# The product of edge weight and one-hot, for building the hop matrix, moved from VectorE to ScalarE

## The reference

```
h = relu(layernorm(x)); x = x + normalize(segment_sum(h[src] @ W_msg + b) + h @ W_self + b')   # layer 0
h = relu(layernorm(x)); x = x + segment_sum(h[src] @ W_rel[edge_type])                         # layer 1
h = relu(layernorm(x)); emb, acc = h, h                                                        # layer 2
for _ in range(3):
    emb = segment_sum(edge_weight[:, None] * emb[src], dst); acc = acc + emb
x = x + acc / 4
h = relu(layernorm(x)); x = x + edge_mlp_layer(h, edge_attr, ...)                              # layer 3
```

## Time and profile before

| | |
|---|---|
| time, median of 3 runs | 9690.01 us (9684.74 to 9692.3) |
| time of the profiled execution | 9684.6 us |
| its span | 9682.9 us |
| VectorE busy over the span | 4792.0 us (49%) |
| ScalarE busy over the span | 1117.6 us (12%) |
| TensorE, mean granted clock over the span | 0.603 of full |

### The profile page before, as it was taken

One profiled execution on the slowest core, in us unless ns is written; L12 is line 12 of the kernel. 1 busy time (PEld: TensorE's weight loads), 2 busy tenths in 40 slices (PEclk: granted clock), 3 DMA queues, 4 the chain that ended last, 5 costly groups with the idle time before them and its releaser, 6 DMA issues.

```text
span 9682.9 us, 125475 instructions
## 1 busy us (share of the span) xinstructions
PE 7196.8 (74%) x38567; PEld 5277.0 (54%) x38568; DVE 4792.0 (49%) x10473; ACT 1117.6 (12%) x2676; POOL 5005.8 (52%) x5265
## 2 busy tenths in 40 slices
PE   2477777777778763333334777777999999999999
PEld 1366666666664663333332222223777777777777
DVE  2599999999992972222222000001444444444444
ACT  1111111111122110000000000001111111111111
POOL 0376666666642767777774111110655555555554
PEclk9555566556655555555556999998555555555555
DMA  5654444445443531111115999996222222222222
GB/s 105 94 96 95 96 96 94 94 95 97 94 87 131 98 75 26 26 26 26 26 26 192 426 403 426 402 426 276 62 60 58 60 58 59 59 58 59 59 60 50
DMA packets 841613, 1176.30 MB, mean 121 GB/s; under 512 B 676431, under 2 KB 696335, under 8 KB 813858
## 3 DMA queue, kind: packets, MB, share of 16 engines
q1 hardware_dynamic: 668850, 923.61, 29.5%
q0 software_dynamic: 172528, 250.20, 12.0%
HBM read 921.76 MB, written 258.23 MB: 122 GB/s over the span
## 4 chain that ended last, share of the span: by engine, by line
PE 40%; DVE 19%; POOL 13%; DMA 13%; issue 13%; DVEq 2%; SPq 1%; ACT 0%; POOLq 0%; ACTq 0%
POOL arena L470 13%; DMA arena<-B_d 10%; PE ps L932 8%; PE ps L875 8%; DVE ps L1178 6%; DVE arena L1179 5%; PE ps L890 4%; PE ps L873 4%; PE ps L951 4%; PE ps L923 4%; DVE arena L1181 4%; DVE pair L1154 3%; PE ps L944 2%; PE ps L773 2%; PE ps L816 2%
## 5 line engine op out<-in xcount | busy, mean ns | idle before, releaser
L470 POOL DMA_INDIRECT arena<-tab,idx x4992 | 4757.9, 953 | 3001.9 <-issue 1582.2
L816 PE MATMUL ps<-arena 128*128 128x64 f32 x6656 | 1400.0, 398 | 1066.2 <-DMA arena<-tab,idx 1064.1
L802 PE MATMUL ps<-arena 128*64 128x98 f32 x15872 | 1457.3, 359 | 696.6 <-DVE arena L1181 695.2
L816 PEld LDWEIGHTS ps<-arena 128*128 128x128 f32 x6656 | 1338.9, 307 | 1136.2 <-issue 1064.9
L802 PEld LDWEIGHTS ps<-arena 128*64 128x64 f32 x15872 | 1181.5, 211 | 938.1 <-DVE arena L1181 794.5
L890 PE MATMUL ps<-arena,ev 128*64 128x512 f32 (+1 forms) x4836 | 1106.4, 603 | 369.7 <-DMA arena<-B_d 294.3
L1154 DVE TENSOR_TENSOR X<-X,ps 128x64 f32 x1664 | 368.1, 221 | 1536.5 <-PE ps L816 1154.3
L890 PEld LDWEIGHTS ps<-arena,ev 128*64 128x64 f32 x4836 | 385.4, 143 | 1090.5 <-issue 738.9
L1179 DVE TENSOR_TENSOR arena<-arena,ps 128x784 f32<-128x784 f32 x992 | 956.9, 965 | 0.0
L932 PEld LDWEIGHTS ps<-arena 128*128 128x128 f32 x3328 | 725.8, 331 | 334.4 <-issue 331.6
L875 PEld LDWEIGHTS ps<-pair,arena 128*128 128x128 f32 x3328 | 725.0, 330 | 312.9 <-issue 312.9
(11 more groups left out here) (201 smaller groups left out, 4406.2 us busy)
## 6 DMA issues: line engine op xcount, KB each, us to landing
arena<-B_d SPq DMA_DIRECT2D x186, 3136.0 KB, 17.1
B_d<-stg SPq DMA_DIRECT2D x248, 784.0 KB
arena<-tab,idx POOLq DMA_INDIRECT x4992
arena<-rel_d SPq DMA_DIRECT2D x208, 256.0 KB, 3.3
tab<-arena SPq DMA_DIRECT2D x26, 1024.0 KB, 3.9
attr_s<-arena SPq DMA_DIRECT2D x13, 512.0 KB, 12.2
attrG<-attr_s SPq DMA_DIRECT2D x208, 32.0 KB, 2.9
rec_d<-arena SPq DMA_DIRECT2D x6, 832.0 KB, 23.9
```

The lines of the kernel that those rows point to most:

```text
L470: pool.indirect_dma_start(gat[:, r, k * width:(k + 1) * width], None, table, bass.IndirectOffsetOnAxis(ap=idx[:, r, k:k + 1], axis=0)).the ...
L802: ins = pe.matmul(ps[3 + j % 2][a * KP:(a + 1) * KP, i2 * KC:(i2 + 1) * KC], Lw[:, j % 2, t, :], Rc[:, j % 2, t, :], start=True, stop=True)
L816: ins = pe.matmul(ps[6 + r % 2][:, k * D:(k + 1) * D], S[:, r % 2, k, :], gat[:, r, k * D:(k + 1) * D], start=True, stop=True)
```

## The change

VectorE no longer multiplies the first one-hot by the edge weights. ScalarE does it in `weighted`, in eight ACTIVATEs (function Copy) for a part, one for each of its eight record tiles, with the weight as a factor for each partition. It reads the one-hot from the PSUM bank and writes Lw. The function is called for part 0 ahead of the loop over a quarter's parts, and for part j + 1 ahead of `matrix_part` of part j, so that it stands in ScalarE's order behind the idx copy of the quarter and before L633 of the part ahead.

VectorE's first one-hot now waits for `lhs_ok` up to the part two back (whose copies read that PSUM bank), its second one for `bmm` as before; the second one signals a new semaphore, `rc_ok`, and TensorE waits for it beside `lhs_ok`, which ScalarE now signals.

```diff
+            def weighted(c, h, r, j):
+
+                u = c * SUBS + (r * QS + j)
+                act.wait_ge(s_["ohp_ok"], u + 1)
+                wait(act, s_["bmm"], u - 1)
+                ohp = ps[2 + 3 * (j % 2)][:].rearrange("p (s k) -> p s k", s=G)
+                s0 = 2 * P + (r * QS + j) * G
+                for t in range(G):
+                    ins = act.activation(Lw[:, j % 2, t, :], ohp[:, t, :], ACT.Copy, scale=cols[:, h, s0 + t:s0 + t + 1])
+                ins.then_inc(s_["lhs_ok"], 1)
...
                         if build:
+                            weighted(c, h, r, 0)
                             for j in range(QS):
+                                if j + 1 < QS:
+                                    weighted(c, h, r, j + 1)
                                 matrix_part(c, r, j)
...
                 pe.wait_ge(s_["lhs_ok"], c * SUBS + (r * QS + j + 1))
+                pe.wait_ge(s_["rc_ok"], c * SUBS + (r * QS + j + 1))
...
+                wait(dve, s_["lhs_ok"], u - 1)
+                dve.tensor_tensor(ohp, column(0, KP), iota_view(0, KP), ALU.is_equal).then_inc(s_["ohp_ok"], 1)
                 wait(dve, s_["bmm"], u - 1)
-                dve.tensor_tensor(ohp, column(0, KP), iota_view(0, KP), ALU.is_equal).then_inc(s_["ohp_ok"], 1)
-                dve.tensor_tensor(Rc[:, j % 2, :, :], column(1, KC), iota_view(0, KC), ALU.is_equal)
-                dve.wait_ge(s_["ohp_ok"], u + 1)
-                dve.tensor_tensor(Lw[:, j % 2, :, :], ohp, column(2, KP), ALU.mult).then_inc(s_["lhs_ok"], 1)
+                dve.tensor_tensor(Rc[:, j % 2, :, :], column(1, KC), iota_view(0, KC), ALU.is_equal).then_inc(s_["rc_ok"], 1)
```

More of the change, by code:

```diff
@@ L221, in gnn_kernel @@
             proj_mv nrm_in nrm_out idx_ok pc_ok rec2_out beg_oh beg_ps off_in off_ps tile_in tile_ps iota_ok
-            tix_ok row_d wm_ok recT cols_ok ohp_ok lhs_ok bmm bev l1_done emb_ok emb_out hop_mm sum_ok ev_a ev_d
+            tix_ok row_d wm_ok recT cols_ok ohp_ok rc_ok lhs_ok bmm bev l1_done emb_ok emb_out hop_mm sum_ok ev_a ev_d
             hop_T ag_a ag_d
```

## The result

| | before | changed |
|---|---|---|
| time, median | 9689.9 us | 9801.0 us |
| lowest to highest of 4 runs | 9684.7 to 9692.3 | 9795.6 to 9816.6 |
| profiled execution, its span | 9682.9 | 9799.0 |

The change makes the kernel slower: ratio 1.0118, 95% interval 1.0100 to 1.0136, that is 111 us. The forecast was slower by 242 us (9932), with a range from 9680 to 10150.

A forecast was written before the change was run, and what follows sets the result against it. VectorE was taken to bound the build at 47.8 us a chunk. The new ring gives 51.9, so 62 chunks add 254 us; less 10 for TensorE's clock, that is 9932 us, range 9680 to 10150.

The forecast's parts named there:

- the ring: Per quarter: ScalarE waits for segment products, weights, TensorE multiplies the parts, then the next segment products; 51.9 us a chunk.
- w0: ScalarE's eight ACTIVATEs weighting part 0, behind the idx copy; claimed from 0.32 to 2.02 us after the segment products' end.
- the relief: VectorE loses 992 L1181 of 0.60 us, 2.4 us a quarter; 420 us less if nothing else moved in.
- w1: ScalarE's eight ACTIVATEs weighting part 1; claimed to end 3.72 us after the segment products' end.
- w2: ScalarE's eight ACTIVATEs weighting part 2; claimed to end 5.81 us after the segment products' end.
- w3: ScalarE's eight ACTIVATEs weighting part 3; claimed to end at 7.90 us, last result at 8.00, after the segment products' end.
- second wait, rc_ok: TensorE's added wait for VectorE's second one-hot, counted in the ring at 0.1 us a quarter.
- I take 10 us off: TensorE's clock: runs at the higher level may become somewhat commoner; 10 us off, giving 9932.
- if L816's mean falls well under 3.2: Sign that the prediction is wrong: segment products averaging well under 3.2 us; 3.17 was taken.
- The cover: VectorE's work between waits fits in its slack; L1159 to L1164 and its 3 us loop return lie mostly inside.
- The operand's read hides: Rival: ScalarE's factor read adds nothing to the pitch, eight ACTIVATEs take 0.88 us, TensorE sets the ring; 9390 us; 11%.
- TensorE warms: Rival: part 3 and L816 run at TensorE's higher clock level, a chunk of 45 us, some 9500 us; 4%.

The follow-up runs named there:

- Experiment 4: The kernel before with L1181 left out and the first one-hot written straight to Lw, edge weights left out: 9314.0 us, ratio 0.9619.
- experiment 10: The changed kernel with the idx copy and its wait moved behind the weighting of part 0 only: 9476.6 us, 0.9771 of the kernel before.
- Experiment 1: The changed kernel with the idx copy and its wait moved behind the weighting of parts 0 and 1: 9438.9 us, 0.9749 of the kernel before.
- experiments 2: The changed kernel with nine ACTIVATEs a part instead of eight, the extra one writing an unread spare tile: 10101.6 us, 1.0431 of the kernel before.
- experiment 5: The changed kernel with four small unread products on TensorE between a quarter's segment products and part 0: 9732.6 us, 1.0062 of the kernel before.
- experiment 3: The changed kernel with an immediate factor 1.0 instead of the per-partition operand, edge weights left out: 9312.5 us, 0.9618 of the kernel before.
- kernel 6: The changed kernel with two of a part's eight record tiles weighted on VectorE, idx copy still first: 9508.0 us, 0.9824 of the kernel before.
- kernels 7: The changed kernel with two of eight tiles weighted on VectorE and the idx copy behind w1: 9435.0 us, 0.9751 of the kernel before.
- 9: The changed kernel with one of eight tiles weighted on VectorE and the idx copy behind w1: 9381.2 us, 0.9678 of the kernel before.
- 11: The changed kernel with one of eight tiles weighted on VectorE and the idx copy behind w0: 9368.1 us, 0.9667 of the kernel before.

## Why the prediction was right and where it was wrong

**Right: VectorE bound the build**, and once it is relieved the gathers stand next at 10.3. Experiment 4 shows it: 9314, where the prediction's 420 us off the profiled 9685 give 9265 for a build at exactly the gathers' pace.

**Right: the ring.** The prediction said that ScalarE's idx wait puts w0 behind the segment products, and that this outweighs the relief. Experiment 1 shows it by moving the wait behind w0 and w1, experiment 10 by moving it behind w0 alone. The two engines' loads (735 and 697 of 1000) bound nothing.

**Wrong in size: the terms of the ring.** Means over 161 quarters of the changed kernel between 600 and 2600 us, from the end of L816 (after: L831):

| step | predicted | measured |
|---|---|---|
| first ACTIVATE of w0 | 0.32 | 0.38 (mostly 0.28) |
| one ACTIVATE to the next | 0.213 | 0.199 |
| w0 to w1 | 1.70 | 1.59 |
| w1 to w2 (with L633 and its wait for part 0) | 2.09 | 2.27 |
| w2 to w3 | 2.09 | 1.95 |
| part 3 starts | 8.06 | 8.07 |
| second wait, rc_ok | 0.10 | 0 |
| part 3 | 1.46 | 1.32 |
| segment products begin, with L793's share | 9.85 | 9.48 |
| segment products | 3.17 | 2.94 |
| quarter | 12.97 | 12.42 |

All that ScalarE does up to part 3 came out within 0.01 us, but by errors that cancel, which is luck: the ACTIVATEs follow each other more closely (16 in 3.40 us), L633 waits for part 0 instead of coming just right, and w0 starts 0.06 later. The step that failed is what follows it, the working for TensorE: "a part is 488.2/335 = 1.46 us on average", "263.7/83.3 = 3.17 us on average" and "I take 10 us off" for the clock. Both means were taken from the kernel before, where L816 and the parts were not in the ring, and were held as if the engine's clock belonged to the instruction. Part 3 and the segment products, 4.63 us in the sum, measured 4.26: 0.37 x 248 quarters = 92 us, where 10 were allowed. The prediction had named the sign for it: "if L816's mean falls well under 3.2". Half of part 3's share was there to be read before: 1.46 is the mean of all four parts, and part 3 alone took 1.39 in the kernel before (167 quarters between 600 and 2600 us). That the two shorten because the clock is higher is in their durations: a part at 0.89 and at 1.57 us, segment products from 1.90 to 3.68, in the same kernel. That the clock answers to the ring's timing is what experiments 2 and 5 show from both sides: a ring 0.54 longer lowered it and cost 0.7 more, fillers raised it and gave 54 to 68 us back. Why a given quarter runs at one level or the other is not shown. The mean over the whole stretch (0.59 before, 0.62 after) hides this: what counts is the clock during part 3 and L816 alone.

The allowance for rc_ok, 0.1 x 248 = 25 us, was the second miss: TensorE's part 3 starts 0.05 us after w3's last result, as before behind L1181. A further 0.14 a quarter is in the start of L816 (after: L831): 0.07 before part 3's modelled end where no transposes stand between, and the transposes add 0.15 on average, not 0.23. Against these, the prediction's sum has a slip of its own: its terms 8.06, 1.46, 0.1 and 3.17 give 12.79, where it wrote 12.75, so with L793 the column of terms adds up to 13.02 and the 12.97 was 0.05 too low. Together 0.37 + 0.10 + 0.14 - 0.01 - 0.05 = 0.55, or 136 us. The sum before the 10 for the clock was 254; less 136 it is 118, against 116 in the spans, of which 107 lie in the build, and 111 in the medians.

**The operand's price.** The Trainium skill, "ScalarE: Activation LUTs", section "What ACT_TABLE_LOAD costs", has 93 ns for each pointer operand and 93 ns of overlap. The first agrees with experiment 3 (0.20 against 0.10 us in the pitch, from 0.198 and 0.105); by its fixed part of 280 ns the pitch would be 0.24, an estimate from that page, and the trace has 0.20, with 314 ns for the first of a row, where the earlier trace rows gave 313. The sum had it from the rows.

**The cover.** VectorE's slack was there (1472.66 of 2000 busy), though not in every quarter: in 16 of 161 w0 waits for its one-hot, 4.2 us in all. One thing in it was seen otherwise: its loop's return, 3.00 us of idle time before L1140, is not hidden in slack but gone: in the changed kernel L1155, the same one-hot, has 4.1 us of such idle time in 1000, where L1140 had 30.7 (the rows below, the kernel before first). In kernel 6, whose VectorE has more instructions in the loop again, it is back at 2.96 before L1155, and kernels 7, 9 and 11 have it too (2.9 to 3.3 us), which is some 0.37 a quarter.

```profile
L1140 DVE TENSOR_TENSOR arena<-relT,ps 128x1024 f32<-128x1024 f32 x83 | 101.4, 1221 | 34.0 <-issue 30.7 <-PE ps L816 3.1
```

```profile
L1155 DVE TENSOR_TENSOR arena<-relT,ps 128x1024 f32<-128x1024 f32 x80 | 97.7, 1221 | 4.3 <-issue 4.1
```

ScalarE's own return to its loop's start was put under L816 by the prediction and called largely hidden. It is, but not quite. Once in eight quarters, where the segment products took 2.00 us, idx started 0.8 to 1.1 us after their end instead of 0.12: 13 times in the some 20 loops of the stretch, which makes 0.07 a quarter or 17 us in all, part of w0's 0.38. That this is the return is inferred from its place, every eighth quarter. One of them, with idx 0.92 behind the end of L831:

```profile
840.62 2.00 PE L831 MATMUL ps<-arena 128*128 128x64 f32 x16
840.74 0.49 ACT L644 COPY stg<-ps 128x392 f32<-128x392 f32 x1 [0.62 <-PE ps L817]
...
843.54 0.20 ACT L657 COPY idx<-srcT 128x8 int32 x1 [2.31 <-PE ps L831]
```

**The rivals.** "The operand's read hides" was priced at 9390; experiment 3, which makes it true, gives 9312, so the sign was right and the condition was not met. What then binds was not as priced: the gathers at 10.3, not TensorE at 10.5. Its threshold of 0.18 us was not tested; no run has a pitch between 0.10 and 0.20. (The "ring of 11.7 with L793" beside it is the one without L793; with it, 47.8/4 is 11.95.) "TensorE warms" was given 4% as a way to a gain, for which over half of all part 3s and L816s had to run at the higher level. It came in part: with 5.25 us at the lower level (1.57 + 3.68) and 2.89 at the higher (0.89 + 2.00), the measured 4.26 is some four tenths of them, an estimate from these durations. As a partial effect it was the largest single error.

## What to carry to other kernels

Before moving work to an idle engine, write down what that engine waits for just ahead of the new work: an engine that was busy 12% of the time can still be late, if its order has a wait for the very engine that then waits for it. Here one wait moved behind two calls turned a loss of 1.2% into a gain of 2.5%. And where TensorE enters a ring, take its durations at either clock level and bound the sum by both; a mean from a stretch in which it was off the path is not its price on the path.

## What was not expected of the hardware

- The same ring with 0.54 us more on ScalarE ran with a granted clock of 0.52 instead of 0.62, and with fillers in TensorE's idle slot at 0.71; added TensorE work made the kernel faster (experiment 5). With no idle slot ahead, the same fillers left the clock at 0.65 (0.64 without). By what rule it rises stays open.
- Eight small ACTIVATEs with a per-partition factor cost 0.20 us each, with an immediate 0.10 (128x64, out of PSUM).
- A TENSOR_SCALAR of 128x64 with two per-partition operands takes 340 ns on VectorE, a TENSOR_TENSOR of the same size (L1169) 221.
